# Second layer's second feed-forward product from three bf16 parts, its results added one group later

## The reference, cut to what matters

```python
xn = _layernorm(x)
x = x + attention(xn) + ffn(xn)
# attention: q, k, v from xn; softmax(q k^T / 16) v; output projection
# ffn: 256 -> 1024 -> 256 with weights that are -1, 0 or 1 after quantisation
h = gelu(einsum('bsd,fd->bsf', xn, w1q) + b1)
y = einsum('bsf,df->bsd', h, w2q) + b2
```

## Time and profile before

| | |
|---|---|
| median of 3 runs | 1538.44 us (1538.16 to 1541.44) |
| profiled execution's own time | 1543.86 us |
| span of the profile | 1542.1 us |
| second layer's TensorE work in the profile | 608.7 to 882.4 us |
| PE busy over the span | 1307.8 us (85%) |
| DVE, ACT, POOL busy over the span | 916.1, 550.9, 363.9 us |
| granted TensorE clock, mean | 0.913 of full speed |

### The profile page before, as it was taken

One profiled execution on the slowest core, in us unless ns is written; L12 is line 12 of the kernel. 1 busy time (PEld: TensorE's weight loads), 2 busy tenths in 40 slices (PEclk: granted clock), 3 DMA queues, 4 the chain that ended last, 5 costly groups with the idle time before them and its releaser, 6 DMA issues. The chain is left out here.

```text
span 1542.1 us, 21651 instructions
## 1 busy us (share of the span) xinstructions
PE 1307.8 (85%) x7315; PEld 815.9 (53%) x7315; DVE 916.1 (59%) x1809; ACT 550.9 (36%) x917; POOL 363.9 (24%) x346
## 2 busy tenths in 40 slices
PE   5776888898889777799999898999767889989996
PEld 3444545564555455566666644445453455544564
DVE  6876576656676775343312368889877453556344
ACT  1465256535653560222321233432422313233320
POOL 3157112211224143510220022201127000000044
PEclk9886999999999867999999989999858899999998
DMA  9232204220312221400000060000002010111123
GB/s 358 62 108 83 58 25 117 63 67 25 113 37 58 56 83 62 132 0 1 0 0 0 15 231 1 0 1 1 0 12 91 31 35 28 38 38 59 55 65 96
DMA packets 72081, 88.86 MB, mean 58 GB/s; under 512 B 19174, under 2 KB 55334, under 8 KB 71337
## 3 DMA queue, kind: packets, MB, share of 16 engines
q1 hardware_dynamic: 65836, 70.78, 15.0%
q0 software_dynamic: 6144, 16.79, 3.4%
HBM read 61.14 MB, written 26.38 MB: 57 GB/s over the span
## 5 line engine op out<-in xcount | busy, mean ns | idle before, releaser
L397 PE MATMUL l_banks<-l_xnT,all_region_a 128*128 128x512 f32 x288 | 129.4, 602 | 0.0
L913 POOL TENSOR_TENSOR all_region_b<-all_region_b,l_lc 128x512 f32<-128x512 f32 x64 | 89.3, 1415 | 121.7 <-DMA all_region_b<-l_lc_rows 121.5
L1926 PE MATMUL l_banks<-l_xnT,mid_region_c 128*128 128x512 f32 (+1 forms) x192 | 92.9, 636 | 11.2 <-DVE l_xnT L2155 9.7
L397 PEld LDWEIGHTS l_banks<-l_xnT,all_region_a 128*128 128x128 f32 x288 | 54.6, 193 | 61.7 <-issue 60.5
L397 PE MATMUL l_banks<-all_region_b,l_xp 128*32 128x32 f32 x2048 | 35.3, 213 | 50.0 <-DVE all_region_b L1182 44.5
L397 PE MATMUL l_banks<-all_region_a,all_xa 128*128 x234 | 70.7, 429 | 4.1 <-DVEq L1241 2.8
L745 ACT ACTIVATE all_region_b<-all_region_b 128x512 f32<-128x512 f32 x64 | 69.4, 1084 | 4.9 <-PE l_banks L397 0.7
L1926 PEld LDWEIGHTS l_banks<-l_xnT,mid_region_c 128*128 128x128 f32 (+1 forms) x192 | 36.4, 195 | 60.0 <-issue 49.5
L397 PEld LDWEIGHTS l_banks<-all_region_b,l_xp 128*32 128x32 f32 x2048 | 29.1, 125 | 70.8 <-DVE all_region_b L1182 38.3
L1182 DVE TENSOR_TENSOR all_region_b<-all_region_b,l_cbd 128x512 f32<-128x512 f32 x64 | 55.5, 869 | 16.7 <-ACT all_region_b L745 12.7
L2824 POOL TENSOR_TENSOR l_rstd<-l_moments,all_neg_half 128x4 f32<-128x4 f32 x12 | 12.4, 1034 | 221.4 <-DVE l_moments L2884 221.2
(11 more groups left out here) (469 smaller groups left out, 2864.0 us busy)
## 6 DMA issues: line engine op xcount, KB each, us to landing
all_region_b<-l_lc_rows SPq DMA_DIRECT2D x256, 64.0 KB
all_xa<-slots_in SPq DMA_DIRECT2D x39, 128.0 KB, 2.1
slots_out<-all_xa SPq DMA_DIRECT2D x39, 128.0 KB, 1.8
mid_vector_rows<-slots_in SPq DMA_DIRECT2D x39, 128.0 KB, 2.1
slots_out<-all_region_a SPq DMA_DIRECT2D x39, 128.0 KB, 1.7
slots_in<-l_xp SPq DMA_DIRECT2D x4, 1024.0 KB, 12.7
all_region_a<-l_gate_up SPq DMA_DIRECT2D x1, 4096.0 KB, 15.4
all_x<-x SPq DMA_DIRECT2D x4, 512.0 KB, 5.6
```

The lines of the kernel that those rows point to most:

```text
L397: return nc.tensor.matmul(out, lhsT, rhs, start=start, stop=stop, **kw)
L913: nc.gpsimd.tensor_tensor(bc[:, k, :, :], bc[:, k, :, :], spread(lc[:, c, heads], 1, BLK), ALU.subtract).then_inc(dd_ready.sem, 1)
L1926: return nc.tensor.matmul(out, lhsT, rhs, start=start, stop=stop)
```

## The change

The second product `d` is made from three bf16 parts of the hidden values and a bf16 copy of the weights. ScalarE applies the Gelu twice to each block, once in float32 (`hT`) and once in bf16 (the first part, `hb[:, 0]`). VectorE makes the middle and the last part of each block from the difference. TensorE's `d` of a group is moved behind the `v` of the next group, and of the second group of a sequence behind the scores of tile 0. VectorE's additions to `x` move with it. The copies of the next group's `xnT` stand behind the last Gelu on ScalarE, and within the loop over the blocks on VectorE. The fourth group's expert rows are added in the first sequence's attention, at tile 2, and GpSimd adds the bias of group 1 before it takes the power for group 3. `hT` and `prob` move into a region that the first layer's weights leave free.

The core of the diff:

```diff
+    hT, prob, left = room(FFN_BLK, GROUP), room(2, SEQ), room(2, GROUP)
+    hb = sb("hb", [P, 3, FFN_BLK, GROUP], BF16)
+    w2_b = sb("w2_b", [P, FFN_BLK, DIM], BF16)
...
@@ TensorE
+            def down(hf):
+                pe.wait_ge(hidden_ready.sem, hidden_ready.done(b, (hf + 1) * FFN_BLK - 1))
+                for t in range(GT // 2):
+                    jobs.wait_room(pe, b, ("d", hf, t))
+                    for i in range(2):
+                        tok = slice((2 * t + i) * P, (2 * t + i + 1) * P)
+                        for f in range(FFN_BLK):
+                            for n in range(3):
+                                last = mm(jobs.bank(("d", hf, t))[:, i * DIM:(i + 1) * DIM], hb[:, n, f, tok],
+                                          w2_b[:, f, :], f == 0 and n == 0, f == FFN_BLK - 1 and n == 2)
+                    jobs.fill(last, ("d", hf, t))
...
+                if hf > 0:
+                    down(hf - 1)
                 pe.wait_ge(parts_ready.sem, parts_ready.done(b, hf))
...
-                pe.wait_ge(h_ready.sem, h_ready.done(b, (hf + 1) * FFN_BLK - 1))
-                for t in range(GT // 2):
-                    ... float32 product from hT and w.w2
...
             scores(0)
+            down(HALVES - 1)
@@ ScalarE
-                    nc.scalar.activation(hT[:, f, :], jobs.bank(("f", hf, f)), ACT.Gelu,
+                    nc.scalar.activation(hT[:, f, :], jobs.bank(("f", hf, f)), ACT.Gelu, bias=col("b1", f))
+                    nc.scalar.activation(hb[:, 0, f, :], jobs.bank(("f", hf, f)), ACT.Gelu,
                                          bias=col("b1", f)).then_inc(h_ready.sem, 1)
                     jobs.free(act.drain(), ("f", hf, f))
+                    if f == FFN_BLK - 1 and hf + 1 < HALVES:
+                        take_xnT(hf + 1)
@@ GpSimd
         power(2)
+        add_bias(0, 1)
         power(3)
-        add_bias(0, 1)
@@ VectorE
                     if b == 0 and hf == 1:
-                        for n in (2, 3):
-                            add_chosen(n)
-                            statistics(n)
+                        add_chosen(2)
+                        statistics(2)
                     jobs.wait_filled(dve, b, ("xnT", hf, 1))
                     norm((b * HALVES + hf + 1) // HALVES, (hf + 1) % HALVES)
+                if hf > 0:
+                    down_add(hf - 1)
+                elif b == 0:
+                    nc.vector.tensor_copy(w2_b[:, :, :], w.w2)
+                for f in range(FFN_BLK):
+                    if f == (1 if b == 0 else FFN_BLK - 2) and hf + 1 < HALVES:
+                        take_xnT(hf + 1)
+                    dve.wait_ge(h_ready.sem, h_ready.done(b, hf * FFN_BLK + f))
+                    nc.vector.tensor_tensor(left[:, f % 2, :], hT[:, f, :], hb[:, 0, f, :], ALU.subtract)
+                    dve.drain()
+                    nc.vector.tensor_copy(hb[:, 1, f, :], left[:, f % 2, :])
+                    dve.drain()
+                    nc.vector.tensor_tensor(hb[:, 2, f, :], left[:, f % 2, :], hb[:, 1, f, :], ALU.subtract).then_inc(
+                        hidden_ready.sem, 1)
...
+                if qt == 0:
+                    down_add(HALVES - 1)
+                if b == 0 and qt == 2:
+                    add_chosen(3)
+                    statistics(3)
```

More of the change, by code:

```diff
@@ L1481, in layer1 @@
     v = mem.xa[:, GT:GT + HB_TILES, :]
-    hT = sb("hT", [P, FFN_BLK, GROUP])
-    prob = sb("prob", [P, 2, SEQ])
+    room = Taker(mem.region_a)
+    room.at = DK * (D_IN + N_EXP) + FFN_BLK * DIM
+    hT, prob, left = room(FFN_BLK, GROUP), room(2, SEQ), room(2, GROUP)
+    hb = sb("hb", [P, 3, FFN_BLK, GROUP], BF16)
+    w2_b = sb("w2_b", [P, FFN_BLK, DIM], BF16)
     pT = sb("pT", [P, 2, HB_TILES, P])
@@ L1498, in layer1 @@
     at = 0
+    down_jobs = [[("d", hf, t) for t in range(GT // 2)] for hf in range(HALVES)]
     for hf in range(HALVES):
@@ L1501, in layer1 @@
         names += [("q", hf, k) for k in range(DK)] + [("v", hf, t) for t in range(GT // 2)]
-        names += [("f", hf, k) for k in range(FFN_BLK)] + [("d", hf, t) for t in range(GT // 2)]
+        if hf > 0:
+            names += down_jobs[hf - 1]
+        names += [("f", hf, k) for k in range(FFN_BLK)]
         for n in names:
@@ L1510, in layer1 @@
     order += score_jobs(0)
+    order += [(n, 6 + i) for i, n in enumerate(down_jobs[HALVES - 1])]
     for qt in range(HB_TILES):
@@ L1529, in layer1 @@
     h_ready = Event(sem("l1_h_ready"), FFN_BLK * HALVES)
+    hidden_ready = Event(sem("l1_hidden_ready"), FFN_BLK * HALVES)
     nmax_ready = Event(sem("l1_nmax_ready"), HB_TILES)
@@ L1630, in _, with take_xnT @@
         with act.Fori(0, BATCH) as b:
+            def take_xnT(hf):
+                jobs.wait_filled(act, b, ("xnT", hf, 1))
+                nc.scalar.activation(xnT[:, 1, hf * GROUP:(hf + 1) * GROUP], jobs.bank(("xnT", hf, 1)),
+                                     ACT.Copy).then_inc(xnT_act.sem, 1)
+                jobs.free(act.drain(), ("xnT", hf, 1))
             for hf in range(HALVES):
                 half = slice(hf * GROUP, (hf + 1) * GROUP)
-                jobs.wait_filled(act, b, ("xnT", hf, 1))
-                nc.scalar.activation(xnT[:, 1, half], jobs.bank(("xnT", hf, 1)), ACT.Copy).then_inc(xnT_act.sem, 1)
-                jobs.free(act.drain(), ("xnT", hf, 1))
+                if hf == 0:
+                    take_xnT(0)
                 for m in range(DK):
@@ L1758, in _, with take_xnT, down_add @@
         for b in range(BATCH):
+            def take_xnT(hf):
+                jobs.wait_filled(dve, b, ("xnT", hf, 0))
+                nc.vector.tensor_copy(xnT[:, 0, hf * GROUP:(hf + 1) * GROUP], jobs.bank(("xnT", hf, 0))).then_inc(
+                    xnT_dve.sem, 1)
+                jobs.free(dve.drain(), ("xnT", hf, 0))
+            def down_add(hf):
+                dve.wait_ge(bias_added.sem, bias_added.done(b, hf))
+                for t in range(GT // 2):
+                    jobs.wait_filled(dve, b, ("d", hf, t))
+                    at = b * HB_TILES + hf * GT + 2 * t
+                    xt = x[:, at:at + 2, :]
+                    last = nc.vector.tensor_tensor(xt, xt, jobs.bank(("d", hf, t)).rearrange(
+                        "p (t d) -> p t d", t=2), ALU.add)
+                    jobs.free(last, ("d", hf, t))
             for hf in range(HALVES):
[L1760 to L1763, removed]
+                if hf == 0:
+                    take_xnT(0)
                 dve.wait_ge(xnT_act.sem, xnT_act.done(b, hf))
```

## The result

| | before | after |
|---|---|---|
| median | 1539.28 us | 1560.79 us |
| runs | 1538.16 to 1541.44 (4) | 1557.13 to 1566.59 (4) |
| ratio, with 95% interval | | 1.0135 [1.0118, 1.0153] |
| span of the profile | 1542.1 us | 1564.8 us |
| granted TensorE clock, mean | 0.913 | 0.899 |

The change costs 21.5 us. It was forecast to cost 10 to 12, with 1564 us as the price of one rival, the lock-out of VectorE by GpSimd: that VectorE's instructions stand still while GpSimd's run.

What follows compares the result with a forecast made beforehand. TensorE's order bounds the second layer. First sequence 2.6, second 1.9 and slow clock 5.7 sum to 10.2 us more, giving 1548.6 or 1554.1 by the baseline's gap; 1550.5 was taken, range 1540 to 1565.

Steps and rivals of the forecast that it cites:

- rival (a): Second sequence: GpSimd's one-operand instructions block VectorE, whose first block waits to 777.4; q +13.7 us, 1564 us; chance 0.13.
- The step that failed: Second sequence, first group: GpSimd's one-operand instructions only slow VectorE's blocks, 0.2 to 0.5 us each; q starts at 779.3.
- The second product: TensorE's `down`: 96 bf16 passes take 10.5 us, 3.5 less; with the Gelu wait gone, 4.3 us saved per group.
- Rival (e): TensorE's `down`: weight loads don't hide; up to 5.2 us more each, four times, 21 us: 1571; chance 0.04.
- VectorE's block: Difference, cast, difference on VectorE: 1.92 us a block, 1.73 without drains; eight take 15.4 us against TensorE's 10.5.
- Rival (d): VectorE's block is cheaper, every 0.1 us moving 3 us; at 1.3 us a block 1530; chance 0.13.
- First sequence: Second layer: TensorE waits for VectorE's list; scores(1) ends at 699.3 against 696.7, +2.6 us at full clock.
- Second sequence without the lock-out: Second layer: TensorE idles 7 us before q, 4.5 us before down(1); end 829.1 against 827.2, +1.9 us.
- The attention: `add_chosen(3)` and its statistics, 5.6 us, go into a round with 5 us free on VectorE: 0, at most 1 us.
- The slow clock: TensorE's clock falls behind three new gaps of 4 us and more: 2.0 + 2.0 + 1.7 = 5.7 us.
- rival (c): The slow clock stays away: 1541.8 us, less if VectorE's list is shorter; chance 0.16, half within 0.2%.
- Rival (b): Unnamed late release returns at the second group's `xnT` while gathers are issued: up to 8.5 us more, 1559; chance 0.08.

Runs made afterwards that it cites:

- e1: Changed kernel with GpSimd's dequantisation of the next layer's weights issued ahead of its last bias addition, in the first sequence's attention; 1538.77 us, ratio 1.0108 to the kernel before.
- e3: Control: the kernel before with the same early dequantisation as e1; 1520.2 us, ratio 0.9991 to the kernel before.
- e4: Changed kernel without the last of VectorE's three instructions a block, TensorE taking the second part twice; 1527.13 us, ratio 1.0040 to the kernel before.
- e5: Changed kernel without VectorE's splitting, TensorE multiplying the first part three times; 1510.8 us, ratio 0.9939 to the kernel before.
- e8: Changed kernel, dequantisation early, bias additions late, third group's results, statistics and normalisation in the first attention, xnT copy two blocks earlier; ratio 1.0029 to the kernel before.
- set B: Set of runs on one chip: both kernels again, e6 and e8; the kernel before had a median of 1540.13 us there.
- e10: e8 with scores(1) ahead of down(1), third group's results added in round 0, cast of w2 ahead of the v copies; 1519.53 us, ratio 0.9989.
- sets A and C: Two sets of runs, each on one chip, A with e1, e3, e4, C with e5, e10, e11; medians of the kernel before 1521.25 and 1521.53 us.
- e11: e10 with VectorE's splitting done for pairs of blocks; 1518.95 us, ratio 0.9986 to the kernel before.
- e6: Changed kernel with early dequantisation, the second sequence's second bias addition late, and splitting in pairs of blocks; 1542.08 us, ratio 1.0011 to the kernel before.

## Why the prediction was right, and where its sum was short

Direction and range held; the likeliest case, 1550.5, was 10 us too low. That the range held is owed to its upper end, which took in the price of rival (a), a case with a chance of 0.13. The second sequence makes up the difference: 5.6 us were forecast for it, slow clock included, and 16.1 measured.

- **The step that failed** is the second sequence's, in the prediction's words: "Beside such ones VectorE's TENSOR_SCALAR is only slowed, 1.02 us for two: I add 0.2 to 0.5 us per block." In its place the GpSimd instructions of L1734 to L1741 held four of VectorE's until they ended, 11.9 us on top of the 2.0 beside the bias addition; e1 takes these instructions away and gets 13.2 us back, 0.9 of it in the clock of q, and e3 shows that they cost nothing by themselves. Rival (a) named this mechanism and priced it at 13.7 us. It put it down to VectorE getting no turn at all; in fact the engines take turns, and it comes to somewhat less: q started 38.0 us after the sequence's first transposes, where the forecast had 27.6 and rival (a) 41.3. By the Trainium skill, page SBUF — State Buffer, "Who interferes with whom", two kinds of VectorE instructions and those of GpSimd keep each other out for a whole instruction, and the one that is issued first goes first: those with both inputs in SBUF, beside a GpSimd instruction that reads SBUF, and those in a two-port mode, which a cast or a copy can enter. The differences at 3.4 us and the casts at 3.5 to 3.85 us agree. Rows 8 were the wrong precedent: they are of another form on both engines. Why those were not held, no run here shows. The prediction's own numbers were loose there too: six blocks of 1.92 us from 765.6 end at 777.1 without any slowing, and with 0.2 to 0.5 us more for each between 778.3 and 780.1, not between 777.1 and 779.5.
- **The second product**: 10.64 us for 96 bf16 passes against 10.5 reckoned; right. Rival (e) is out.
- **VectorE's block**: 1.87 us against 1.92; right. Rival (d) is out, and so is its rule of what a cheaper block would bring: for 0.77 us less on each of sixteen blocks, 12.3 us, e4 gets 15.3 us in the first sequence, because the slow clock goes too.
- **First sequence**: 2.6 at full clock and 2.0 of slow clock, 4.6 forecast, 4.15 measured. That it came so close is in part luck, two misses against each other: `down(1)` began 75.3 us after the first transposes, where 76.6 were reckoned, and the slow clock in it took 2.8 us. The 1.7 us of slow clock in `down(0)` cost nothing, because VectorE, whose blocks `down(1)` then waited for, did not wait for TensorE in that stretch. The sum also hid a loss: it was made against a profile with the 9.46 us gap, which the changed kernel doesn't have. Against a kernel before without it (e3) the change loses 14.1 us there. That 17 us of saving would remain available was never true in this sequence: e5 gets 1.6 of 8.6 us.
- **Second sequence without the lock-out**: 1.9 plus 3.7 of slow clock forecast, 3.0 measured in e1, with 3.2 of slow clock in it (q 5.22 instead of 3.69 us, `down(1)` 12.32 instead of 10.64).
- **The attention**: 0 to 1 us forecast, 0.2 measured. That holds for round 2; e8 shows that the same work in round 1 costs 3.75 us.
- **The slow clock** behind new gaps: right in place, 2.8 us in the first sequence's `down(1)` and 2.4 and 1.7 in the second sequence, where 2.0, 2.0 and 1.7 were reckoned. So rival (c) is out.
- **Rival (b)**, the late release: not seen in either profile of the changed kernel.
- **The median against the profile**: both profiles of the unchanged kernel before, on chips where its median is 1539 to 1540, have the gap. The first of the two readings, that all executions have it, was the right one to lean to. In set B the three changed kernels measure 2 to 4 us more against the kernel before than their stretches and the attention between them say. Their profiles show it behind the second layer, from the end of the second sequence to the end of the kernel: 716.2, 715.5 and 714.7 us, where the kernel before takes 712.6. So it need not mean that some executions of the kernel before lack the gap; why the rest takes longer was not tested. What releases the copy so late, and why only some chips show it, stays open.

## What to carry to other kernels

Before VectorE gets new instructions that work within SBUF, look at what GpSimd runs in that stretch: not only whether VectorE had time there, but how long each GpSimd instruction is, since one instruction of VectorE can wait that long (3.9 us here). In this kernel the long weight preparation on GpSimd held nobody beside VectorE work that reads PSUM (e1).

When a product is made shorter, ask what it covered. Here the f32 product hid the normalisation of the next group and VectorE's lag, and its shorter form gave most of the saving back in the first sequence. A lag that comes from two rates, 1.87 us a block on VectorE against 1.3 on TensorE, isn't cured by emptying the list; it wants other work between, as in e10.

## What was not expected of the hardware

The kernel before takes 1521 us in sets A and C and 1539 to 1540 in set B and in the runs of the result. Of the 18.8 us between the traced spans of e3 (set A) and of the kernel before in set B, 12.1 are in the first sequence; 9.1 of them are the longer wait ahead of q (10.01 against 0.87 us), with VectorE and ScalarE released 8.6 us after the transposes have ended and 2.9 us after GpSimd has issued the last gather. The gathers alone don't explain it: in e3 they run from 628.8 to 649.8 us, and the copies start in the midst of them, at 641.5 us on VectorE. Another 2.3 us lie ahead of the layer and 4.4 behind its second sequence.

And at the same place and with the same gap of 2.28 us the clock fell in e11 (mean granted clock 0.67 over q) and stayed up in e10 (1.00). Timelines of PE, e11 and then e10:

```profile
758.27 5.37 PE L1555 MATMUL l_banks<-l_xnT,all_xa 128*128 128x512 f32 x8 [2.28 <-issue]
```

```profile
763.01 3.67 PE L1555 MATMUL l_banks<-l_xnT,all_xa 128*128 128x512 f32 x8 [2.28 <-issue]
```

At this place it also fell in e8 (gap 2.27 us, q 5.25) and stayed up in e5 (2.26 us, 3.67) and even in e6 (3.70 us, 3.70). So one such gap makes the time of a kernel uncertain by 1.6 to 1.7 us, and two variants that differ by no more than that in a stretch can't be told apart by one profile.
